# Last batch of an attention kernel: transposes two blocks ahead in two PSUM banks, late products on GpSimd, five column groups

## The reference, cut to what matters

```python
q = heads(x @ W_q); k_t = heads(text @ W_k); v_t = heads(text @ W_v)
probs_t = softmax(q @ k_t.T * scale)
text_out = probs_t @ v_t
attn_scores = q @ k_ip.T * scale
qsem = l2norm(probs_t @ text)            # 512 wide, for each head and query
sem = qsem @ l2norm(ip).T
probs_ip = softmax(attn_scores + 0.5 * sem) * mask
out = (text_out + probs_ip @ v_ip) @ W_out + b_out + x
```

## Time and profile before

| what | us |
|---|---|
| median of 3 runs | 732.73 |
| lowest, highest | 730.79, 734.06 |
| the profiled execution's own time | 731.94 |
| its span, first to last instruction | 730.1 |
| PE, DVE, ACT, POOL busy | 713.3, 634.2, 558.5, 422.1 |
| a steady batch | about 43 |
| from `transposes(1)` of the last batch to its last product | 36.3 |
| from there to the last instruction | 11.4 |

### The profile page before, as it was taken

How to read it: one execution, slowest core, us unless ns; L and a number is a source line. 1 busy time by engine, 2 the same in 40 slices (tenths; PEclk the granted TensorE clock), 3 DMA queues, 4 the chain that set the end, 5 groups by cost and what they waited for, 6 DMA issues and landing times.

```text
span 730.1 us, 22544 instructions
## 1 busy us (share of the span) xinstructions
PE 713.3 (98%) x7221; PEld 560.9 (77%) x7221; DVE 634.2 (87%) x1878; ACT 558.5 (76%) x1595; POOL 422.1 (58%) x524
## 2 busy tenths in 40 slices
PE   8898999999999999999999999999999999999897
PEld 6577788787787878788787777878787887877665
DVE  5588998989889898988999898898989989898986
ACT  5478787877878788787877878787887878777772
POOL 7545646465564745656565565656556564654754
PEclk9999999999999999999999999999999999999999
DMA  9764372442536246263543436354352725325001
GB/s 277 164 142 99 79 140 73 83 125 45 120 75 135 74 62 144 41 128 75 107 104 58 105 80 133 76 88 113 51 117 73 142 71 92 64 43 123 13 1 22
DMA packets 136355, 68.57 MB, mean 94 GB/s; under 512 B 76672, under 2 KB 136112, under 8 KB 136240
## 3 DMA queue, kind: packets, MB, share of 16 engines
q1 hardware_dynamic: 131856, 64.05, 41.1%
q10 hardware_dynamic: 4064, 2.73, 1.3%
q0 software_dynamic: 320, 0.36, 0.4%
HBM read 40.38 MB, written 15.24 MB: 76 GB/s over the span
## 4 chain that ended last, share of the span: by engine, by line
PE 91%; DVE 2%; DMA 2%; ACT 1%; issue 1%; POOL 1%; SPq 0%; ACTq 0%; DVEq 0%; POOLq 0%
PE ps_gram L785 18%; PE ps_prep L673 18%; PE ps_pT L768 13%; PE ps_gram L786 12%; PE ps_score L760 6%; PE ps_prep L734 5%; PE ps_val L794 4%; PE ps_val L795 2%; PE ps_prep L731 1%; PE ps_prep L704 1%; PE ps_prep L706 1%; PE ps_prep L824 1%; PE ps_prep L835 1%; DMA w_raw<-in_L_xattn_W_k_ip 1%; DMA q_st<-q_bounce 1%
## 5 line engine op out<-in xcount | busy, mean ns | idle before, releaser
L592 POOL TENSOR_TENSOR dual<-prob 128x371 f32<-128x371 f32 (+1 forms) x288 | 251.3, 872 | 288.1 <-ACT prob L1043 288.1
L785 PE MATMUL ps_gram<-gram_hi,pT_hi 125*128 125x371 f16 (+1 forms) x864 | 272.3, 320 | 0.1
L786 PE MATMUL ps_gram<-gram_lo,pT_hi 125*128 125x371 f16 (+2 forms) x864 | 230.1, 267 | 0.0
L1037 ACT ACTIVATE pT_hi<-ps_pT 125x384 f16<-125x384 f32 (+1 forms) x288 | 138.9, 482 | 113.5 <-PE ps_pT L768 105.4
L1235 DVE TENSOR_TENSOR pT_lo<-ps_pT,pT_hi 125x384 f16<-125x384 f32 (+1 forms) x288 | 155.2, 539 | 33.0 <-ACT pT_hi L1037 28.2
L1027 ACT ACTIVATE prob<-ps_score,low 128x371 f32<-128x371 f32 (+1 forms) x288 | 165.3, 574 | 21.6 <-DVE low L1230 16.4
L1230 DVE TENSOR_REDUCE low<-ps_score 128x1 f32<-128x371 f32 (+1 forms) x288 | 154.9, 538 | 18.8 <-PE ps_score L760 13.7
L1248 DVE CUSTOM_DVE_ANT_0 quad_junk<-ps_gram,dual 128x371 f32<-128x371 f32 (+1 forms) x288 | 153.1, 532 | 4.5 <-PE ps_gram L786 1.6
L794 PE MATMUL ps_val<-val,pT_hi 125*128 125x84 f16 (+3 forms) x864 | 152.3, 196 | 0.0
L1043 ACT ACTIVATE prob<-prob 128x371 f16<-128x371 f32 (+1 forms) x288 | 151.5, 526 | 0.0
L768 PE MATMUL ps_pT<-ident,prob 128*125 128x128 f32 (+1 forms) x864 | 142.2, 273 | 6.5 <-ACT prob L1027 3.2
(11 more groups left out here) (264 smaller groups left out, 1468.4 us busy)
## 6 DMA issues: line engine op xcount, KB each, us to landing
ctx_sb<-in_ctx_t SPq DMA_DIRECT2D x15, 750.0 KB, 5.0
w_raw<-k_bounce SPq DMA_DIRECT2D x32, 216.0 KB, 4.0
k_st<-k_bounce SPq DMA_DIRECT2D x28, 216.0 KB, 3.8
k_bounce<-k_hi SPq DMA_DIRECT2D x15, 288.0 KB, 4.3
k_bounce<-k_lo SPq DMA_DIRECT2D x15, 288.0 KB, 4.4
q_st<-q_bounce SPq DMA_DIRECT2D x60, 63.0 KB, 2.4
xt_sb<-in_x_t SPq DMA_DIRECT2D x16, 168.0 KB, 4.7
w_raw<-k_hi SPq DMA_DIRECT2D x32, 84.0 KB, 3.1
```

The source lines that it names most:

```text
L592: nc.gpsimd.tensor_tensor(dual[0:r, t % 2, :], prob[0:r, g % 4, 0:TX], prob_16[0:r, t % 2, :], ALU.subtract).then_inc(s_dual, 1)
L785: nc.tensor.matmul(ps_gram[t % 2][:, 0:TX], hi, gh[0:TROWS[i], i, :], start=(i == 0), stop=False, skip_group_check=True)
L786: last = nc.tensor.matmul(ps_gram[t % 2][:, i * TC:TX], hi, gl[0:TROWS[i], i, i * TC:TX], start=False, stop=(i == NT - 1), skip_group_chec ...
```

## The change

All of it concerns the last batch (b = 15) and the tail; the other batches issue the same instructions in the same order.

Transposes go two blocks ahead, odd blocks into `ps_prep[1]` and even ones into `ps_pT`; what used `ps_prep[1]` in this batch (the ip turn, batch 14's finish) uses `ps_prep[0]`. ACT and DVE get loops of their own (`last_body`). In ACT's, `exps(t+3)` and `halve(t+1)` come first and `probs_hi(t+2)` last. In DVE's, `probs_lo(t+2)` comes last, behind `quadratic(t)`. The ip steps become 1, 1, 2, 6, 7, the finish steps 10, 12, 14, 16. Five of batch 14's token products (k = 4, 5, 6, 7, 9) go from DVE to POOL. Columns 0 to 15 get their sums, norms and roots in three portions during the batch (three of the four norm operations on POOL), and the tail keeps columns 16 to 19. `ps_val`'s fourth group is cut in two. In the tail DVE does `soft` 4 to 9 before `attn_lo`, and the third pad is 3 matmuls for 9.

```diff
 GROUPS = ((0, 6), (6, 12), (12, NBX), (NBX, NB))
+LAST_GROUPS = (*GROUPS[:3], (NBX, NBX + 2), (NBX + 2, NB))
...
-BUSY = (14, 5, 9, 2)
-LAST_TURN_STEP, LAST_SPLIT_STEP, LAST_MAKE_STEP, LAST_TAKE_STEP = 2, 3, 5, 6
+BUSY = (14, 5, 3, 2)
+LAST_TURN_STEP, LAST_SPLIT_STEP, LAST_MAKE_STEP, LAST_TAKE_STEP = 1, 2, 6, 7
...
+LAST_EARLY = ((0, 6), (6, 12), (12, 16))
+LAST_HALVES = (1, 2, 4)
+LAST_LATE = LAST_EARLY[-1][1]
+LAST_VALS_STEP, LAST_SUM_STEP, LAST_NORM_STEP, LAST_POW_STEP = {8: 0, 12: 1, 16: 2}, {9: 0, 13: 1, 16: 2}, {10: 0, 14: 1, 17: 2}, {11: 0, 15: 1, 17: 2}
+LAST_FINISH_STEP, LAST_RESIDUAL_STEP = {10: 0, 12: 1, 14: 2, 16: 3}, 9
...
-SOFT_LATER = 1
+LAST_SOFT_POOL = {4: (4, 5), 5: (6, 7), 6: (9,)}
+LAST_EXP_STEP, LAST_TEXT_OUT_STEP, LAST_SOFT_POW_STEP = 7, 7, 3
...
+LAST_SOFT_AT = {(t + 1, place): k for (t, place), k in SOFT_AT.items() if k < 4}
+LAST_SOFT_AT.update({(6, 0): 8, (8, 0): 10, (8, 1): 11, (8, 2): 12})
...
+def groups(b):
+    return GROUPS if b.n < B - 1 else LAST_GROUPS
...
+        def turned(b, t):
+
+            return ps_prep[1] if b.n == B - 1 and t % 2 else ps_pT
+
+        def finish_bank(f, k):
+
+            return ps_prep[(k + 1) % 2 if f.n < B - 2 else 0]
...
+            def soft_products(f, k):
...
+                pair = nc.gpsimd.tensor_tensor
+                pool.wait_ge(s_soft, SOFT * f.n + k)
...
+                else:
+                    last = pair(fused[:, :, :], fused[:, :, :], over_ip(fmax[:, 0, :]), ALU.subtract)
+                last.then_inc(s_soft, 1)
...
+            def last_early(b, step):
+                if step in LAST_VALS_STEP:
+                    n = LAST_VALS_STEP[step]
+                    pool.wait_ge(s_half, len(GROUPS) * b.n + LAST_HALVES[n])
+                    pool.wait_ge(s_text_out, b.n)
+                    pool.wait_ge(s_soft, SOFT * (b.n - 1) + SOFT_ARGS)
+                    sum_values(*LAST_EARLY[n]).then_inc(s_early, 1)
+                if step in LAST_NORM_STEP:
...
+                    h0, h1 = LAST_EARLY[n]
+                    r, v = rsum[:, h0:h1], nrm[:, :, h0:h1]
+                    pool.wait_ge(s_early, EARLY_STEPS * (b.n + n) + 2)
+                    pool.wait_ge(s_quad, NB * b.n + h1)
+                    nc.gpsimd.tensor_tensor(v[:, 0, :], meta[b.odd][0:S, h0:h1, 0], r, ALU.mult).then_inc(s_early, 1)
+                    pool.wait_ge(s_early, EARLY_STEPS * (b.n + n) + 3)
+                    nc.gpsimd.tensor_tensor(v[:, 1, :], v[:, 0, :], r, ALU.mult).then_inc(s_early, 1)
+                    pool.wait_ge(s_early, EARLY_STEPS * (b.n + n) + 4)
+                    nc.gpsimd.tensor_scalar(v[:, 2, :], v[:, 1, :], 2.0 / G_DOWN, EPS * EPS, ALU.mult, ALU.max).then_inc(s_early, 1)
+                if step in LAST_POW_STEP:
+                    n = LAST_POW_STEP[step]
+                    pool.wait_ge(s_early, EARLY_STEPS * (b.n + n + 1))
+                    inverse_roots(*LAST_EARLY[n])
...
+                    if not prepare and t == NB - 2:
+                        last_early(b, t)
...
-                    end_early(b, t, prepare)
+                    if prepare:
+                        end_early(b, t)
+                    else:
+                        if t != NB - 2:
+                            last_early(b, t)
+                        for k in LAST_SOFT_POOL.get(t, ()):
+                            soft_products(b.last(), k)
...
-                end(b.last(), VALS_STEP)
-                inverse_roots(*EARLY_POWS[NB - 1])
-                end(b.last(), POW_STEP)
+                f = b.last()
+                pool.wait_ge(s_half, len(GROUPS) * f.n + len(LAST_GROUPS))
+                pool.wait_ge(s_moved, MOVED * B)
+                sum_values(LAST_LATE, H).then_inc(s_vals, 1)
+                pool.wait_ge(s_soft, SOFT * f.n + SOFT_NORMS)
+                inverse_roots(LAST_LATE, H)
...
-                reached(pe, s_pT_lo, g)
+                if b.n < B - 1 or t == 0:
+                    reached(pe, s_pT_lo, g)
+                elif t == 1:
+                    pe.wait_ge(s_prep_lo, NM * B)
+                else:
+                    pe.wait_ge(s_pT_lo, g - 1)
...
+                if t == groups(b)[group(b, t)][0]:
...
-                    reached(pe, s_half, len(GROUPS) * b.n + group(t))
+                    reached(pe, s_half, len(GROUPS) * b.n + group(b, t))
...
+                bank = finish_bank(f, k)
...
+                if k < NF - 1 or f.n == B - 2:
                     reached(pe, s_fin_ev, NF * f.n + k)
+                if k == 0 and f.n == B - 2:
+                    pe.wait_ge(s_vip_out_ev, 1)
...
-                    if t + 1 < NB:
+                    if not prepare:
+                        if t == 0:
+                            transposes(b, 1)
+                        if t + 2 < NB:
+                            transposes(b, t + 2)
+                    elif t + 1 < NB:
                         transposes(b, t + 1)
-                    elif prepare:
+                    else:
                         transposes(b.next(), 0)
...
+                    if not prepare and t in LAST_FINISH_STEP:
+                        finish(b.last(), LAST_FINISH_STEP[t], NM * B)
...
+                if not prepare:
+                    return last_body(b)
...
+            def last_body(b):
+                for t in range(NB):
+                    if t == 0:
+                        probs_hi(b, 1)
+                    if LAST_FINISH_STEP.get(t) == 2:
+                        attn_out(b.last())
+                    if t + 3 < NB:
+                        exps(b, t + 3)
+                    if t + 1 < NB:
+                        halve(b, t + 1)
+                    if t == LAST_TURN_STEP:
+                        take_vip_T()
+                    if t == LAST_TAKE_STEP:
+                        take_vip_out()
+                    if t == LAST_EXP_STEP:
+                        fin_exp(b.last())
+                    if t + 1 == groups(b)[group(b, t)][1]:
+                        half_out(b, group(b, t))
+                    if t + 2 < NB:
+                        probs_hi(b, t + 2)
+                store(b.last())
...
+            def last_sums(b, n):
+
+                dve.wait_ge(s_early, EARLY_STEPS * (b.n + n) + 1)
+                dve.wait_ge(s_text_out, b.n)
+                norms(b, 0, *LAST_EARLY[n]).then_inc(s_early, 1)
...
+                    last = norms(f, k, EARLY if f.n < B - 1 else LAST_LATE, H)
...
-                    dve.wait_ge(s_rn, POWS * (f.n + 1))
+                    dve.wait_ge(s_rn, POWS * (f.n + 1) if f.n < B - 1 else POWS * f.n + len(LAST_EARLY) + 1)
...
+            def last_body(b):
+
+                def softly(t, place):
+                    if (t, place) in LAST_SOFT_AT:
+                        soft(b.last(), LAST_SOFT_AT[t, place])
+
+                for t in range(NB):
+                    if t + 3 < NB:
+                        minimum(b, t + 3)
+                    softly(t, 0)
+                    if t == 0:
+                        probs_lo(b, 1)
+                    if t in LAST_FINISH_STEP:
+                        finish(b.last(), LAST_FINISH_STEP[t])
+                    softly(t, 1)
+                    quadratic(b, t)
+                    softly(t, 2)
+                    if t + 2 < NB:
+                        probs_lo(b, t + 2)
+                    if t in LAST_SUM_STEP:
+                        last_sums(b, LAST_SUM_STEP[t])
...
+                for k in range(SOFT_NORMS, SOFT_ARGS):
+                    soft(f, k)
                 dve.wait_ge(s_last_hi, 1)
...
-                for k in range(SOFT_NORMS, SOFT_ARGS):
-                    soft(f, k)
```

More of the change, by code:

```diff
@@ L101, in rows, with group @@
     return P if t < NBX else S
-def group(t):
-    return next(n for n, (t0, t1) in enumerate(GROUPS) if t0 <= t < t1)
+def groups(b):
+    return GROUPS if b.n < B - 1 else LAST_GROUPS
+def group(b, t):
+    return next(n for n, (t0, t1) in enumerate(groups(b)) if t0 <= t < t1)
 def column(t):
-    return (t - GROUPS[group(t)][0]) * BW
+    return (t - next(t0 for t0, t1 in GROUPS if t0 <= t < t1)) * BW
 def place(a, k):
@@ L918, in turn_vip @@
                 for c in range(CC):
-                    last = nc.tensor.transpose(ps_prep[1][0:channels(c), c * VR:(c + 1) * VR],
+                    last = nc.tensor.transpose(ps_prep[0][0:channels(c), c * VR:(c + 1) * VR],
                                                vip_diag[:, B - 1, c * P:c * P + channels(c)], ident[0:VR, 0:VR])
@@ L1045, in half_out @@
             def half_out(b, n):
-                t0, t1 = GROUPS[n]
+                t0, t1 = groups(b)[n]
                 r, w = rows(t0), BW if t0 < NBX else 2 * VW
@@ L1123, in body @@
                         probs_hi(b, t + 1)
-                    elif prepare:
+                    else:
                         probs_hi(b.next(), 0)
-                    if not prepare and t == LAST_TURN_STEP:
-                        take_vip_T()
-                    if not prepare and t == LAST_TAKE_STEP:
```

(14 more changed lines are left out.)

51 lines of the change are left out of this document (29 added, 22 removed).

## The result

The changed kernel is slower. Its median is 741.89 us over 6 runs, against 734.4 us (also 6 runs) for the kernel before. The two medians divide to 1.0102; the ratio on record is 1.0125, with a 95% interval of 1.0101 to 1.0149. The forecast was 740.4. The profiled execution took 741.4 us (span 739.6), 9.46 more than the one before (731.94). Cut at two events of the trace, that difference is as follows.

A forecast was written before the change was run, and what follows sets the result against it. It took a 1.83 us ring through the single bank to set the last batch's plain steps, the rest stalls. 731.94 + 7.3 (batch) + 0.4 (tail) = 739.6, forecast as 740.4 for the runs' median; range 736.5 to 745.

The forecast's parts named there:

- Part 1, the ring: Last batch: exps, halve, probs_hi, probs_lo, next minimum, next exps form a cycle of 2.46 us a step; fourteen turns, 34.3.
- Part 2, the extras: Last batch: small operations inside the ring on ScalarE and VectorE, plus project_vip on TensorE, add 2.7 us (bounds 0 to 4).
- Part 3, the end of the batch: From exps(17) to the last product 5.0 us, with finish(3) now before products(16); last product 7.3 us later than before.
- Part 4, moved products and norms: Last batch: token products, norms and roots moved to POOL are covered by waiting there; they gain and cost nothing.
- Part 5, the tail: After the last product: portion 2 delays POOL's vals, but the last root is shorter; +0.4 us, bounds -0.4 and +1.5.
- A: Rival, last batch: TensorE's pauses drop its clock to 1.2 GHz, 9 us more, 749 us; chance 0.05.
- B: Rival, last batch: minimum not held behind probs_lo, so TensorE's 1.55 us a step rules; faster, 728.4 us; chance 0.07.
- C: Rival, last batch: even and odd block chains run at 1.85 us a step as before; no change, 731 us; chance 0.04.
- D: Rival: the ring rules but all extras and the tail fall low, 737 us; chance 0.80 together with the forecast.

The follow-up runs named there:

- e1: Changed kernel with VectorE doing minimum(t+4) ahead of probs_lo(t+2); 732.62 us, ratio 1.0004 to the kernel before the change.
- e7: Changed kernel with a second halve per step of the last batch on ScalarE, into a buffer nobody reads; 748.7 us, ratio 1.0213.
- e3: Changed kernel with the last batch's old order on TensorE, ScalarE and VectorE and the single bank's wait, all else kept; 733.4 us, ratio 1.0008.
- e11: e1 and e5 together, with attn_lo put back ahead of soft 4 to 9 in VectorE's tail; 731.14 us, ratio 0.9973.
- e5: Changed kernel without the third early portion (columns 12 to 15), left to the tail; 739.61 us, ratio 1.0102.

## Why the prediction was right, and where it was off

**Part 1, the ring: right in mechanism and size.** Forecast 2.46 a turn, measured 2.49; the 0.03 is the link from `exps` to `halve`, 0.53 for 0.50. Cutting one link (e1) ended the 2.49, and lengthening another by 0.40 (e7) made every turn 0.40 longer. What decided was to write down, for the new loops, the cycle through semaphores and places in a queue, and to count by how many blocks it advances.

**Part 2, the extras: forecast 2.7, measured 2.1.** From `exps(3)` to `exps(17)` 36.76 us passed: twelve turns of 2.49 and two of 2.40 (718.76 - 716.36, the one 112-row turn without an extra) make 34.7, the extras 2.1. Single turns show them: 0.29 for `take_vip_T`, 0.48 for each of two `half_out`, 0.47 for `vip_out` and `fexp`, 0.27 for the third `half_out`. `project_vip`'s 0.3 did not appear, nor more than 0.1 of each `last_sums`. As the plain turns were 0.4 longer in sum (34.7 for 34.3), the total came out 0.2 below the forecast (37.0).

**Part 3, the end of the batch: right.** Forecast 5.0 from `exps(17)`, measured 726.42 - 721.43 = 4.99.

**Part 4, moved products and norms: right, as far as shown.** Forecast nothing; e3 has them all, together with the other new steps, and its batch is not longer than before (34.09 for 34.70). No run moves them alone.

**Part 5, the tail: the mis-sized step.** Forecast +0.4, at most +1.5; measured +1.82, above the bound. Two terms carry it. The `vals` I put at 1.8 after the last product start at 2.97. I had let portion 2 begin behind `quadratic(16)`, as if POOL were free then; but the root of portion 1 (1.34) held POOL until 726.42, and `vals` of portion 2 (0.33) and `dual(17)` (0.83) followed before the norms could start. None of these waits for data in the rows above: it is one queue of 5.1 us, which I had looked at only from its last 2. Then the root of four columns took 1.23, not 1.0, and soft 4 came 2.54 after `vals` instead of my 2.15. Together 5.51 - 3.97 = 1.54. The other 0.3 is mostly `attn_lo` standing ahead of `fmax` (forecast +0.3; the distance from `fexp` to `fmax` grew from 0.37 to 0.59, and e11 got 0.22 back by undoing it). e5 showed the first term by taking it away.

**The sum.** 7.05 for 7.3 and 1.82 for 0.4 lie on either side, and the total of both (8.9) is 1.2 above the forecast 7.7. Against the profiled execution the forecast was 739.6 and the time 741.4: these 1.2 and the 0.6 of the late start. That the median of the runs, 741.89, lies only 1.5 above the forecast is in part luck. The step forecast was 7.7 us; the traces show 8.9 from `exps(3)` on, while the medians of the six runs each lie 7.5 apart, because the kernel before came out at 734.4 and not at the 732.73 from which the forecast started.

**The rivals.** A: the granted clock stayed 1.00 through the batch with TensorE stopping about 1 us in every step, so no run here shows in the batch the swing between two clocks of which the Trainium skill ("TensorE: Matmul & The Clock Gate", section "A second HAM failure mode: psum-queue depth-cycling") warns. B named the right condition: with `minimum` no longer behind `probs_lo` (e1) the batch falls to 32.06. It does not fall to TensorE's bare 30.0 (B's 31.6, less 684.04 - 682.40 before `exps(3)`), and with its tail e1 is even with the kernel before. The turn of 2.49 excludes C. D needed extras and tail both on the low side; the extras were (2.1 for 2.7), the tail was not (+1.82).

## What to carry to other kernels

When an order by hand is changed, trace each cycle through semaphores and in-order queues, and divide its start distances by the number of blocks that it advances; the engines' busy shares did not show it, and one swapped pair of instructions was worth 9.7 us here. Before counting on a second buffer, look for what stands unneeded in the queues between its producer and its consumer: the same two banks gave -2.7 us under the old order and, with `minimum` behind `probs_lo`, +7 under the new. Count what is queued on the slow engine over the whole last two steps before adding early work to it: 4 columns made early saved 0.6 us and cost 2.2.
